# Three dense taps of a deformable convolution: position rows and block-pick rows in rings of their own, the first rows loaded ahead of the step table, the batches begun one turn earlier

## What is computed

```python
offset = _conv(data_im, offset_w)            # 18 maps: y and x shift of each of 9 taps
mask = jax.nn.sigmoid(_conv(data_im, mask_w))
y = base_y + off_y; x = base_x + off_x       # where a tap reads, per pixel
y0 = floor(y); x0 = floor(x); ly = y - y0; lx = x - x0
val = w00*gather(y0,x0) + w01*gather(y0,x0+1) + w10*gather(y0+1,x0) + w11*gather(y0+1,x0+1)
out = jnp.einsum('op,bphw->bohw', weight, val * mask)
```

## Time and profile before

| | us |
|---|---|
| three runs, median | 1084.52 |
| three runs, lowest and highest | 1081.42, 1088.95 |
| the profiled execution, device time | 1085.33 |
| its span, first to last instruction | 1083.1 |
| mean granted PE clock, as a share of full | 0.816 |

### The profile page before, as it was taken

One profiled execution on the slowest core, in us unless ns is written; L12 is line 12 of the kernel. 1 busy time (PEld: TensorE's weight loads), 2 busy tenths in 40 slices (PEclk: granted clock), 3 DMA queues, 4 the chain that ended last, 5 costly groups with the idle time before them and its releaser, 6 DMA issues.

```text
span 1083.1 us, 8308 instructions
## 1 busy us (share of the span) xinstructions
PE 808.6 (75%) x2365; PEld 386.9 (36%) x2365; DVE 838.1 (77%) x1161; ACT 386.9 (36%) x544; POOL 580.0 (54%) x528
## 2 busy tenths in 40 slices
PE   3347839577876886778778787838988878879886
PEld 1123214122321244444445353326433333324333
DVE  4989733899998587899998999597857767767765
ACT  1120256745442363111112111003635455555552
POOL 0000000467751378777777777777777765466530
PEclk9658969699998895767876878555989889988987
DMA  4000026000002611121111112735243333233220
GB/s 114 0 0 1 0 63 128 0 1 1 0 1 45 139 49 39 52 53 50 52 50 52 49 52 53 196 88 142 78 128 110 110 102 98 89 104 100 90 83 19
DMA packets 32339, 69.82 MB, mean 64 GB/s; under 512 B 12368, under 2 KB 12624, under 8 KB 31184
## 3 DMA queue, kind: packets, MB, share of 16 engines
q1 hardware_dynamic: 16080, 35.27, 12.1%
q0 software_dynamic: 15360, 31.49, 11.0%
q10 hardware_dynamic: 864, 2.64, 1.1%
HBM read 54.94 MB, written 5.77 MB: 56 GB/s over the span
## 4 chain that ended last, share of the span: by engine, by line
DVE 30%; PE 17%; ACT 12%; issue 8%; DMA 8%; POOL 7%; SPq 3%; DVEq 0%; ACTq 0%; POOLq 0%
DMA UZ<-dense_rows 7%; POOL got L777 6%; ACT scratch L1446 6%; DVE scratch L1171 5%; PE PS L812 4%; DVE scratch L1097 4%; DVE scratch L1178 3%; SPq L1428 3%; DVE prodg L788 2%; PE PS L1054 2%; DVE PS L1094 2%; DVE XN L1454 2%; PE PS L1039 2%; ACT XN L1446 2%; PE PS L1271 2%
## 5 line engine op out<-in xcount | busy, mean ns | idle before, releaser
L777 POOL DMA_INDIRECT got<-corner_table,idx_slot x405 | 403.6, 997 | 162.8 <-issue 118.9
L1469 PE MATMUL PS<-scratch,UZ 128*128 128x512 f32 (+1 forms) x288 | 145.2, 657 | 33.0 <-DVE scratch L1454 33.0
L1039 PE MATMUL PS<-parts,selb 96*128 96x512 bf16 (+1 forms) x256 | 89.0, 448 | 83.6 <-DVE scratch L1097 43.8
L1054 PE MATMUL PS<-scratch,wt 128*128 128x512 f32 x256 | 146.1, 701 | 0.5 <-DVE scratch L1178 0.5
L1454 DVE SCALAR_TENSOR_TENSOR scratch<-scratch,XN 128x512 f32<-128x512 f32 x144 | 90.8, 692 | 71.9 <-ACT XN L1443 71.2
L777 POOL DMA_INDIRECT got<-corner_table,idx_all x75 | 83.9, 1118 | 60.6 <-DVE prime L1345 38.0
L812 PE MATMUL PS<-ln_g,w 128*128 128x32 f32 x576 | 102.2, 345 | 0.0
L812 PEld LDWEIGHTS PS<-ln_g,w 128*128 128x128 f32 x576 | 99.7, 269 | 0.0
L1469 PEld LDWEIGHTS PS<-scratch,UZ 128*128 128x128 f32 (+1 forms) x288 | 57.4, 208 | 115.0 <-issue 98.4
L818 ACT ACTIVATE G<-PS 128x32 f32 (+1 forms) x32 | 6.3, 197 | 249.7 <-PE PS L812 249.6
L1469 PE MATMUL PS<-XN,UZ 128*128 128x512 f32 x144 | 76.8, 689 | 16.6 <-DVE XN L1454 16.6
(11 more groups left out here) (347 smaller groups left out, 1348.2 us busy)
## 6 DMA issues: line engine op xcount, KB each, us to landing
UZ<-dense_rows SPq DMA_DIRECT2D x24, 512.0 KB, 3.3
got<-corner_table,idx_slot POOLq DMA_INDIRECT x405, 2.5
UZ<-dense_rows SPq DMA_DIRECT2D x96, 64.0 KB, 3.4
XN<-ln_g SPq DMA_DIRECT2D x6, 256.0 KB, 5.1
got<-corner_table,idx_all POOLq DMA_INDIRECT x75, 2.5
corner_table<-scratch SPq DMA_DIRECT2D x1, 1056.0 KB, 10.4
corner_table<-XN SPq DMA_DIRECT2D x1, 1056.0 KB, 10.4
X<-in_x SPq DMA_DIRECT2D x4, 256.0 KB, 5.1
```

Of the source, the lines that this page charges most:

```text
L777: pool.indirect_dma_start(got[:, slot, tap, :, :].rearrange("p k c -> p (k c)"), None, tables[b], bass.IndirectOffsetOnAxis(ap=index[:, ta ...
L1039: last = nc.tensor.matmul(PS[:, first + n, :], selb[:, which, j, :], parts[:, bass.ds(i * CHUNK + n * BANK, BANK)], start=True, stop=True)
L1054: last = nc.tensor.matmul(PS[:, 4 + n, :], wt[:, W_SUM:W_SUM + P], dBC[:, j % 2, n * BANK:(n + 1) * BANK], start=False, stop=(j == PAIRS - 1))
L1469: last = nc.tensor.matmul(PS[:, n % 4, :], steps[rows, j, :, :].rearrange("p b c -> p (b c)"), ramps[k][rows, j, :], start=(j == 0), stop= ...
```

## The change

1. The position rows (y and x) keep a ring of three, now of two rows per buffer; the four pick rows get a ring of four (`PICKS`) of their own, `pick_rows`, with semaphores of their own (`load_pick`, early ones used again).
2. `dense_load(n)` waits only for the ramps of batch n - 3; `dense_load_pick(n)` waits for the pick of batch n - 4. SP issues `dense_load(n)`, then `dense_load_pick(n - 1)`. The store of image 0 stands ahead of the rows of batch 5.
3. `dense_scalar(n)` waits only for the position rows (16 instead of 80); `dense_pick(n)` waits for the pick rows.
4. On SP the rows of batch 0 are loaded as soon as the fields are in DRAM, ahead of the copy of the step table.
5. Batch n follows turn 29 + floor(33 n / 24) instead of 30 + floor(32 n / 24).
6. Buffers move so that batch 0 can start while the corner table is still in XN: `ramps[0]` and `ramps[1]` are in scratch, `ramps[2]` in XN, `hats[0]` in UZ, `steps_odd` in scratch. ACT waits for `steps_out` before batch 0, and for both tables before batch 1. Semaphores `iota`, `absd`, `rows_in`, `steps_in` are folded into others; `ramps` now counts 11 a batch.

No arithmetic is added or taken away: the same operations with the same shapes.

```diff
+PICKS = 4
+        load_pick = [(x_in, 64), (vec_in, 32), (rest_in, 32), (mat_in, 16)]
-                 for t in (xn_flat[:, 0:SLOPES * BANK], scratch[:, 0:SLOPES * BANK], scratch[:, SLOPES * BANK:2 * SLOPES * BANK])]
+                 for t in (scratch[:, 0:SLOPES * BANK], scratch[:, SLOPES * BANK:2 * SLOPES * BANK], xn_flat[:, 0:SLOPES * BANK])]
-        loads = [UZ[:, 1024 + 1536 * k:1024 + 1536 * (k + 1)].rearrange("p (r n) -> p r n", r=3) for k in range(RING)]
+        loads = [UZ[:, 1024 + 1024 * k:1024 + 1024 * (k + 1)].rearrange("p (r n) -> p r n", r=2) for k in range(RING)]
+        pick_rows = [UZ[:, 4096 + BANK * k:4096 + BANK * (k + 1)] for k in range(PICKS)]
...
         def dense_first(sp):
             sp.wait_ge(de["rows_out"], 1)
-            sp.dma_start(rows_dram.rearrange("q k n -> (q k) n"), fields_t).then_inc(de["rows_in"], 16)
+            sp.dma_start(rows_dram.rearrange("q k n -> (q k) n"), fields_t).then_inc(de["tables_in"], 16)
+            sp.wait_ge(de["tables_in"], 16)
+
+        def dense_steps(sp):
             sp.wait_ge(de["table_done"], 1)
...
             if n >= RING:
-                sp.wait_ge(de["ramps"], (SLOPES + 1) * (n - RING + 1))
-                sp.wait_ge(de["t_used"], n - RING + 1)
-            sp.dma_start(loads[k][:, 0:2, :], rows_dram[q, 6 * d:6 * d + 2, cols].partition_broadcast(P)).then_inc(load[k], 16)
+                sp.wait_ge(de["ramps"], (SLOPES + 2) * (n - RING + 1))
+            sp.dma_start(loads[k][:, :, :], rows_dram[q, 6 * d:6 * d + 2, cols].partition_broadcast(P)).then_inc(load[k], 16)
+
+        def dense_load_pick(sp, n):
+            half, q, d = BATCHES[n]
+            k, cols = n % PICKS, slice(half * BANK, (half + 1) * BANK)
+            if n >= PICKS:
+                sp.wait_ge(de["t_used"], n - PICKS + 1)
             for i in range(4):
-                sp.dma_start(loads[k][32 * i:32 * i + 32, 2, :], rows_dram[q, 6 * d + 2 + i, cols].partition_broadcast(32)).then_inc(load[k], 16)
+                sp.dma_start(pick_rows[k][32 * i:32 * i + 32, :], rows_dram[q, 6 * d + 2 + i, cols].partition_broadcast(32)
+                             ).then_inc(load_pick[k][0], 16)
...
             if n == 0:
-                act.wait_ge(de["iota"], 4)
-                act.wait_ge(de["table_done"], 1)
+                act.wait_ge(l3["w3_zero"], 5)
+                act.wait_ge(de["steps_out"], 1)
+            elif n == 1:
+                act.wait_ge(de["tables_in"], 32)
                 act.wait_ge(l3["table_in"], 32 * B)
-            act.wait_ge(load[k], 80 * (n // RING + 1))
+            act.wait_ge(load[k], 16 * (n // RING + 1))
...
-            v.wait_ge(load[k], 80 * (n // RING + 1))
+            pick_in, before = load_pick[n % PICKS]
+            v.wait_ge(pick_in, before + 64 * (n // PICKS + 1))
...
-        FIRST_TURN, LAST_TURN = 30, 62
+        FIRST_TURN, LAST_TURN = 29, 62
...
-                for n in range(len(BATCHES)):
-                    if n == 4:
+                for n in range(len(BATCHES) + 1):
+                    if n == 5:
                         store(sp, 0, 0, GROUPS)
-                    dense_load(sp, n)
+                    if n < len(BATCHES):
+                        dense_load(sp, n)
+                    if n == 0:
+                        dense_steps(sp)
+                    if n:
+                        dense_load_pick(sp, n - 1)
```

More of the change, by code:

```diff
@@ L738, in build @@
         knot = sb("knot", [P, SLOPES])
-        de = {n: sem("dense_" + n) for n in ("iota", "rows_out", "rows_in", "steps_out", "steps_in", "table_done", "absd", "ramps",
+        de = {n: sem("dense_" + n) for n in ("rows_out", "tables_in", "steps_out", "table_done", "ramps",
                                              "prods", "t_psum", "t_used", "sum_psum", "added")}
         load = [sem(f"dense_load{k}") for k in range(RING)]
+        load_pick = [(x_in, 64), (vec_in, 32), (rest_in, 32), (mat_in, 16)]
         rows_dram = nc.dram_tensor("dense_rows", (4, C, QUARTER), F32, kind="Internal").ap()
@@ L745, in build @@
         ramps = [t.rearrange("p (j n) -> p j n", j=SLOPES)
-                 for t in (xn_flat[:, 0:SLOPES * BANK], scratch[:, 0:SLOPES * BANK], scratch[:, SLOPES * BANK:2 * SLOPES * BANK])]
-        hats = [xn_flat[:, 4608 + BANK * k:4608 + BANK * (k + 1)] for k in range(RING)]
+                 for t in (scratch[:, 0:SLOPES * BANK], scratch[:, SLOPES * BANK:2 * SLOPES * BANK], xn_flat[:, 0:SLOPES * BANK])]
+        hats = [UZ[:, 6144:6656]] + [xn_flat[:, 4608 + BANK * k:4608 + BANK * (k + 1)] for k in range(RING - 1)]
         picked = [xn_flat[:, 6144 + BANK * k:6144 + BANK * (k + 1)] for k in range(2)]
-        loads = [UZ[:, 1024 + 1536 * k:1024 + 1536 * (k + 1)].rearrange("p (r n) -> p r n", r=3) for k in range(RING)]
-        steps_odd = UZ[:, 1024:2048].rearrange("p (j b c) -> p j b c", j=8, c=C)
+        loads = [UZ[:, 1024 + 1024 * k:1024 + 1024 * (k + 1)].rearrange("p (r n) -> p r n", r=2) for k in range(RING)]
+        pick_rows = [UZ[:, 4096 + BANK * k:4096 + BANK * (k + 1)] for k in range(PICKS)]
+        steps_odd = scratch[:, 8192:9216].rearrange("p (j b c) -> p j b c", j=8, c=C)
         fields_t = UZ[:, 5632:6656]
@@ L1433, in dense_scalar @@
             if n == 0:
-                act.wait_ge(de["iota"], 4)
-                act.wait_ge(de["table_done"], 1)
+                act.wait_ge(l3["w3_zero"], 5)
+                act.wait_ge(de["steps_out"], 1)
+            elif n == 1:
+                act.wait_ge(de["tables_in"], 32)
                 act.wait_ge(l3["table_in"], 32 * B)
-            act.wait_ge(load[k], 80 * (n // RING + 1))
+            act.wait_ge(load[k], 16 * (n // RING + 1))
             if n >= RING:
                 act.wait_ge(de["t_psum"], n - RING + 1)
-            nc.scalar.activation(hats[k], loads[k][:, 0, :], ACT.Abs, bias=negy[:, 0:1]).then_inc(de["absd"], 1)
+            nc.scalar.activation(hats[k], loads[k][:, 0, :], ACT.Abs, bias=negy[:, 0:1]).then_inc(de["ramps"], 1)
             nc.scalar.activation(ramps[k][:, 0, :], loads[k][:, 1, :], ACT.Relu, bias=knot[:, 0:1]).then_inc(de["ramps"], 1)
-            act.wait_ge(de["absd"], n + 1)
+            act.wait_ge(de["ramps"], (SLOPES + 2) * n + 1)
             nc.scalar.activation(hats[k], hats[k], ACT.Relu, bias=1.0, scale=-1.0).then_inc(de["ramps"], 1)
@@ L1452, in dense_weights @@
                 rows = up if j == SLOPES - 1 else slice(0, P)
-                v.wait_ge(de["ramps"], (SLOPES + 1) * n + 2 + j)
+                v.wait_ge(de["ramps"], (SLOPES + 2) * n + 3 + j)
                 nc.vector.scalar_tensor_tensor(ramps[k][rows, j, :], ramps[k][rows, j, :], 1.0, hats[k][rows, :],
@@ L1460, in dense_sample @@
             if n == 0:
-                pe.wait_ge(de["steps_in"], 16)
+                pe.wait_ge(de["tables_in"], 32)
                 pe.wait_ge(l3["below_in"], 4 * B)
@@ L1479, in dense_pick @@
             v.wait_ge(de["t_psum"], n + 1)
-            nc.vector.tensor_tensor(picked[n % 2], PS[:, n % 4, :], loads[k][:, 2, :], ALU.mult).then_inc(de["t_used"], 1)
+            nc.vector.tensor_tensor(picked[n % 2], PS[:, n % 4, :], pick_rows[n % PICKS], ALU.mult).then_inc(de["t_used"], 1)
         def dense_sum(pe, n):
@@ L1550, in _ @@
                     nc.gpsimd.iota(negy[rows, :], [[0, 1]], base=0, channel_multiplier=-1,
[L1551 to L1552 removed]
+                                   allow_small_or_imprecise_dtypes=True).then_inc(l3["w3_zero"], 1)
+                    pool.wait_ge(l3["w3_zero"], 2 * s + 2)
                     nc.gpsimd.iota(knot[rows, :], [[-2, SLOPES]], base=1 - s, channel_multiplier=0,
[L1554 to L1555 removed]
+                                   allow_small_or_imprecise_dtypes=True).then_inc(l3["w3_zero"], 1)
+                    pool.wait_ge(l3["w3_zero"], 2 * s + 3)
                 for c in range(NCHUNK):
```

5 lines of the change are left out of this document (1 added, 4 removed).

## The result

The changed kernel takes 1013.48 us (median of 4 runs, 1012.18 to 1014.29), the kernel before 1085.26 us beside it (4 runs). The ratio is 0.934, 95% interval 0.930 to 0.937: 6.6 per cent faster, 72 us. The forecast was 1017.0, with a range of 1007 to 1047. The profiled execution took 1014.24 us with a span of 1012.0 us.

The account below looks back on a forecast made before the run. The batch loop tied through one shared buffer bound the kernel. POOL's start 752.4, gathers 251.5, landing 2.5 and tail 8.4 end at 1014.8, later than PE's 1008.5; plus 2.2 around the span gave 1017.0 us, range 1007 to 1047.

Parts of the forecast that it names:

- The bound before: Dense batches: a loop tied through one shared buffer, the pick releasing the next loads, one batch in 13.8 us.
- The PE chain: PE's samples, sums and pairs: batch 3 at 782.7, batch 23 at 986.8, end at 1008.5.
- The clock term: PE: the sum has 2.4 GHz throughout; idle PE costs twice, once as idle and once at 1.2 GHz.
- The POOL chain: Gathers of image 1 from 752.4: 192 at 1.31 us are 251.5, then landing 2.5 and tail 8.4, end at 1014.8.
- Turn 29: Start of the dense batches: ACT's batch 0 going one turn earlier gives 4.2 us.
- rival 3: SP's rows really wait for ramps, not the pick: only the turn's 4.2 us gained, time 1081; chance 0.03.
- The early load: SP's rows of batch 0, loaded ahead of the step table: worth 0 of its own.
- The waits that were said to be covered: ACT's later copy of group 29, and SP's store of image 0 ahead of batch 5's rows: each cost 0.
- Rival 1: PE short of work now and then; one batch in three losing 4.4 us gives 1042; chance 0.20.
- Rivals 3 and 4: The fourth: denser DVE and DMA traffic slows POOL's gathers, 1.72 us each making it 1 per cent slower, 1095.4; chance 0.01.
- Rival 2: POOL's gathers slow beside DVE's dense products, 1.46 us on average, time 1046; chance 0.06.

Follow-up runs that it names:

- tied_all: Changed kernel with position and pick rows issued together after the pick of batch n - 3, ACT waiting for both: 1082.85 us, ratio 0.998 to the kernel before.
- tied_rows: Changed kernel with position rows of batch n waiting for the pick of batch n - 3 again, pick rows in their own ring: 1055.79 us, ratio 0.973.
- pool_less: Changed kernel with five instead of six gathers per group of image 1, some 42 us less on POOL: 1010.34 us, ratio 0.933 to the kernel before.
- pe_less: Changed kernel without the matmul of slope 4 in each sample, 21.6 us less on PE: 1011.84 us, ratio 0.935 to the kernel before.
- ring_only: Changed kernel with step table copied and both tables landed ahead of the first rows, batches from turn 30: 1014.63 us, ratio 0.936 to the kernel before.
- turn_28: Changed kernel with the batches from turn 28 instead of 29: 1013.11 us, ratio 0.935 to the kernel before.
- steps_first: Changed kernel with step table copied and both tables landed before the rows of batch 0 are issued, turn 29 kept: 1013.43 us, ratio 0.937.
- tied_by_four: Changed kernel with position rows of batch n waiting for the pick of batch n - 4: 1012.60 us, ratio 0.936 to the kernel before.
- picks_three: Changed kernel with three pick-row buffers instead of four: 1014.08 us, ratio 0.938 to the kernel before.

## Why the prediction was right

**The bound before.** Right: one shared buffer tied the batches to the pick. tied_all brings 13.7 us a batch back, tied_rows 12.6. The 13.8 us were one turn; six turns average 13.7. What was a little short is tied_rows' forecast of some 12 us, made with the prediction's steps: it took the 1.9 us of the pick-row issues off whole, and only 1.1 us of it was there to be had, since the issues ran while the position rows were landing.

**The PE chain.** 20 batches and 14 pairs were put at 204.1 us (9.07 x 20 + 1.62 x 14); batch 3 to batch 23 took 990.18 - 786.42 = 203.8 us. The start was put at 782.7 for batch 3 and came at 786.42, because PE and ACT run 3.3 us later by then: the copy of group 28 on ACT ends the same idle of 3.78 us at 748.51 that it ended at 745.21 before. That part is not touched by the change, and it moves from one execution to the next: PE starts that group at 743.96 in the kernel after, at 740.66 before, and at 737.11 and 736.43 in tied_rows and pool_less, which do the same as the kernel after up to there. POOL does not move with it: its first gather of image 1 stands at 751.60, 752.43, 753.25 and 752.56. With 3.3 added, the predicted end of 1008.5 is 1011.8, and it was 1012.0; the sum could not have known the 3.3, so an agreement to 0.2 us is in part luck. The clock term (2.4 GHz throughout) was right. DVE was put at 9.5 us a batch below it, with 2.3 us for what the prediction calls a pair and is one group, half a pair; the sum uses it as a group and is right, and DVE was busy 179 of 195 us, 9.4 for each 10.2.

**The POOL chain.** 192 gathers were put at 251.5 us, 1.31 each; from 751.60 to the end of the last one at 1002.2 they took 250.6, 1.305 each. What was mis-sized is the landing behind them: I put 2.5 us behind the end of the last gather, but the landing runs from its issue (2.42 us in pe_less, where it ended the wait; here 2.52 from 1000.95 to the product at 1003.47), so the step was 1.25 us too long; with the start 0.8 us earlier and the gathers 0.9 us shorter than forecast that makes the 2.8 us by which 1014.8 missed 1012.0. That POOL's would be "the later one" was not borne out: the two chains end together, within what the trace can tell. The forecast was also set against a median 0.8 us below the execution it was built on; like for like it was 1016.2.

**Turn 29.** It was booked at 4.2 us, the gap between two copies on ACT. For ACT's start that was right: 4.3 us, directly behind the copy of group 28. As the price of the edit it was wrong, in rival 3's 1081 too, since it left out what the start costs further on: a group of image 0 (2.2 us at full clock) moves behind the first batch, which leaves 1.6 us at the end of PE's chain, and POOL's chain gains nothing by it. The times of ring_only and turn_28 are too close to settle this, and would not exclude 4.2 us; the 1.6 us rest on one trace of each kernel. The sum itself carried the moved group, so the forecast was not harmed. The early load at 0 was right within the spread (steps_first).

**The waits that were said to be covered.** The copy of group 29 went to 769.35 instead of 749.48 and cost PE nothing. The store of image 0 held back the rows of batch 5 until 795.38, 8.5 us of idle ACT, and cost nothing either: PE had no gap from 795 to 990. SP's order (pick rows ahead of the next position rows) did not tie the loop: tied_by_four and picks_three, which tie it harder, are not slower.

**The rivals.** Rival 1 (PE short of work, clock lost) did not come: PE waits 2.93 us for DVE at the first batch, as it did before, and has no gap from 795 to 990. Rivals 3 and 4 did not come.

Rival 2, gathers slowed by the products on DVE, did not come: DVE is busy 179 of 195 us, 132 of them in products with two inputs in SBUF (L1466 and L838), and the gathers' mean is 1.305 us, not 1.46. But the prediction's reading that the products L1454 leave the gathers alone rested on one row and was too strong. Before, 17 of the 192 gathers took over 1.1 us, and 9 of these ran beside nothing but L1454, the longest 1.45 us at 936.22. In the kernel after it is 19, three of them beside nothing but L1466, as this one:

```profile
760.10 1.39 POOL L780 DMA_INDIRECT got<-corner_table,idx_all  x1 [0.31 <-issue]
```

```profile
759.41 5.67 DVE L1466 SCALAR_TENSOR_TENSOR scratch<-scratch,XN 128x512 f32<-128x512 f32 x9
```

The other 16 ran beside the rows of a group (L788 to L801, L836 to L848), some of them beside its sums and no longer its product. The gathers with only dense products beside them, 77, took 0.97 us in the mean, where an undisturbed one takes 0.94. The Trainium skill (GPSIMD Engine Reference, Specifications) says that DVE instructions with two SBUF inputs contend with GpSimd for the SBUF interfaces. By that rule the dense products should slow gathers; the trace agrees that they can, but it was rare here: over all 192, slow gathers add 0.06 us to 1.25. Why one gather is slowed and the next is not stays open.

## What to carry to other kernels

When a ring's buffer holds two things that are freed at different stages, the later one sets the pace: add up the steps once around the loop, divide by the number of batches it carries, and compare with the busiest engine's time for a batch; one batch of slack here was worth 43 us (tied_rows against tied_by_four), the next one nothing. Time that PE idles counts about one and a half times here, since 23 us of the 70 were matmuls at the slower clock. And when a change opens one bound, work out the chains of all engines up to the end: two that arrive together make every later edit of one of them worth nothing.

## What the runs showed beyond that

One size changed that nobody had expected to: the DMA that brings 512 KB of position rows to 128 partitions took 3.3 us to land before and 4.1 us after (medians from issue). The busier DMA engines are not the main reason: their share went up from 0.33 to 0.45, but tied_all, with 0.34, has a median of 3.9 already. What else differs is where the rows land, in buffers of two rows instead of three; no run tells whether that is the cause. The longer landing is hidden now.

```profile
UZ<-dense_rows SPq DMA_DIRECT2D x24, 512.0 KB, 4.1
```
